# Two attention passes of a graph network: one-hots of the open nodes compared once, the fall factors finished by ScalarE, and scores less maxima formed by TensorE in PSUM

## The reference, cut to what matters

```python
m = jax.ops.segment_max(score, dst, num_segments=n)
ex = jnp.exp(score - m[dst])
denom = jax.ops.segment_sum(ex, dst, num_segments=n)
agg = jax.ops.segment_sum(ex[..., None] * message, dst, num_segments=n)
out = agg / denom[..., None]
```

## Time and profile before

| | |
|---|---|
| median of 3 runs | 3441.07 us (3435.51 to 3443.51) |
| span of the profiled execution, first to last instruction | 3438.5 us |
| VectorE's adds of pass 1 (416) | from 1399.9 to 1975.9 us |
| VectorE's adds of pass 2 (416) | from 2172.7 to 2737.0 us |
| TensorE busy in the span | 2897.5 us (84%) |
| VectorE, ScalarE, GpSimd busy | 2544.3 (74%), 1935.0 (56%), 2183.2 us (63%) |

### The profile page before, as it was taken

The page is one execution under the profiler, slowest core; times in us unless marked ns, Lnnn a source line. Parts: engine busy times, 40 slices in busy tenths (PEclk is TensorE's granted clock), DMA queues, the critical chain, the costliest instruction groups (busy, mean ns, idle before and its releaser), DMA issues. The chain is left out here.

```text
span 3438.5 us, 60509 instructions
## 1 busy us (share of the span) xinstructions
PE 2897.5 (84%) x15715; PEld 1839.2 (53%) x15715; DVE 2544.3 (74%) x6536; ACT 1935.0 (56%) x6284; POOL 2183.2 (63%) x2289
## 2 busy tenths in 40 slices
PE   5799889999988896788888866899999897788875
PEld 4666555555555553455555544677777653333332
DVE  8899789999977554888888843799999874444444
ACT  0478655555541452687788722688888753333333
POOL 1777677777756532766666355777777314777774
PEclk9999899999999998798899988899999996655665
DMA  5334388888851789777777555777777444333334
GB/s 179 100 104 130 121 256 261 260 265 264 261 138 34 242 324 351 243 229 220 218 209 212 128 186 184 224 227 227 228 228 226 117 199 162 104 103 103 103 104 103
DMA packets 260604, 651.44 MB, mean 189 GB/s; under 512 B 66781, under 2 KB 115626, under 8 KB 253498
## 3 DMA queue, kind: packets, MB, share of 16 engines
q0 software_dynamic: 141840, 474.50, 45.9%
q1 hardware_dynamic: 118442, 173.08, 15.5%
HBM read 505.42 MB, written 145.27 MB: 189 GB/s over the span
## 5 line engine op out<-in xcount | busy, mean ns | idle before, releaser
L2132 POOL DMA_INDIRECT a_rows<-table,met x568 | 560.3, 987 | 241.1 <-issue 137.8
L3729 PE MATMUL ps<-rows_in,hot_w 128*128 128x256 f32 x832 | 431.5, 630 | 114.2 <-ACT hot_w L3691 68.5
L1330 POOL DMA_INDIRECT rows_in<-table,met x416 | 413.1, 993 | 142.9 <-issue 80.3
L3679 POOL DMA_INDIRECT rows_in<-table,met x416 | 404.2, 972 | 144.3 <-issue 118.3
L3754 DVE TENSOR_TENSOR xs<-xs,ps 128x256 f32 x416 | 175.1, 421 | 302.7 <-PE ps L3729 298.1
L3729 PEld LDWEIGHTS ps<-rows_in,hot_w 128*128 128x128 f32 x832 | 192.6, 284 | 353.1 <-ACT hot_w L3691 199.2
L3691 ACT ACTIVATE hot_w<-hot,met 128x128 f32<-128x128 f32 x416 | 166.7, 402 | 372.1 <-PE ps L3729 353.9
L2629 PE MATMUL ps<-a_rows,a_hot 128*128 128x260 f32 x1136 | 316.4, 402 | 18.2 <-DVE acc L2635 12.7
L2132 POOL DMA_INDIRECT xs<-table,met x264 | 258.7, 980 | 107.3 <-issue 61.3
L833 POOL DMA_INDIRECT records<-rec,rows x241 | 260.5, 1081 | 87.6 <-issue 72.9
L2635 DVE TENSOR_TENSOR acc<-acc,ps 128x520 f32 x416 | 287.0, 690 | 34.6 <-PE ps L2629 13.6
(11 more groups left out here) (492 smaller groups left out, 6417.3 us busy)
## 6 DMA issues: line engine op xcount, KB each, us to landing
a_hot_t<-one_hots SPq DMA_DIRECT2D x104, 256.0 KB, 5.0
table<-stage SPq DMA_DIRECT2D x25, 1024.0 KB, 3.9
rows_in<-table,met POOLq DMA_INDIRECT x832, 3.8
one_hots<-hot_t SPq DMA_DIRECT2D x52, 256.0 KB
dst_row<-slot_rows SPq DMA_DIRECT2D x51, 256.0 KB, 5.0
by_dst<-dst_rows SPq DMA_DIRECT2D x25, 512.0 KB, 5.7
by_dst<-lo_rows SPq DMA_DIRECT2D x24, 512.0 KB, 4.4
a_rows<-table,met POOLq DMA_INDIRECT x568, 3.8
```

Of the source, the lines that this page charges most:

```text
L1330: e.indirect_dma_start(self.rows[:, n % self.RING, 0:2 * D], None, self.table, bass.IndirectOffsetOnAxis(ap=self.b.met[:, n, R_SRC:R_SRC + ...
L2132: e.indirect_dma_start(self.row(n, 0, self.width), None, self.table, bass.IndirectOffsetOnAxis(ap=b.met[:, n, self.word:self.word + 1], ax ...
L3679: e.indirect_dma_start(self.rows[:, n % self.RING, :], None, self.table, bass.IndirectOffsetOnAxis(ap=self.b.met[:, n, R_REL:R_REL + 1], a ...
L3729: e.matmul(b.ps[:, n % self.BANKS, 0:D], self.hot_w[:, n % GRP_H, :], self.rows[:, n % self.RING, :], start=True, stop=True).then_inc(self ...
```

## The change

1. `vector_ends` compares the 26 open nodes with all 128 partitions once (`opened[:, 0]`) and keeps one less that beside it (`opened[:, 1]`). The row of nodes is loaded to 128 partitions in place of 8. The comparison in each window on VectorE (`open`) and `other` on ScalarE are gone.
2. `scale_up` is one matmul: a matrix of ones times `diag`, which puts exp(-fall) on all partitions.
3. ScalarE finishes the factor in slot 0: factor = PSUM * opened0 + opened1, from PSUM to SBUF. It waits for `scale_out` (TensorE) and for the `rescaled` of the window before; `rescale` on VectorE waits for it and reads SBUF.
4. "back" on TensorE is two matmuls into one PSUM region in place of a transpose: identity times scores, then the maxima times minus the identity. `below` on VectorE is gone, and ScalarE takes the exponential from PSUM, behind `turned_back`.
5. Turning the scores of window w into the same bank now waits for the exponentials of window w-1 (`exped`), and the write of scores waits for "back" of window w-2.

```diff
 # Segments
-        self.opens = sb("opens", [H2, NW])
+        self.opened = sb("opened", [P, 2, NW])
...
-        e.tensor_copy(self.opens[:, :], self.local_f[:, 0:NCH:WIN]).then_inc(kept, 1)
+        e.tensor_scalar(self.opened[:, 0, :], self.local_f[:, 0:NCH:WIN], b.part_f[:, :], None, ALU.is_equal).then_inc(kept, 1)
         e.wait_ge(kept, 4)
+        e.tensor_scalar(self.opened[:, 1, :], self.opened[:, 0, :], -1.0, 1.0, ALU.mult, ALU.add)
...
-        e.dma_start(self.local_f[:, :], on_all(self.ends[2], H2)).then_inc(self.back, 16)
+        e.dma_start(self.local_f[:, :], on_all(self.ends[2], P)).then_inc(self.back, 16)
 # Attend.constants_vector
+        e.tensor_scalar(self.minus[:, :], b.ident[0:R, 0:R], -1.0, None, ALU.mult)
 # Attend.vector, add
-                e.wait_ge(self.scale_out, self.w0 + w + 1)
+                e.wait_ge(*self.factored.at(w + 1))
                 if n:
                     e.wait_ge(self.added, self.c0 + n)
-                self.rescale(e, tile, b.ps[:, self.SMALL, 128:128 + H]).then_inc(self.rescaled, 1)
+                self.rescale(e, tile, self.factor[:, :]).then_inc(self.rescaled, 1)
 # Attend.vector, chain
-                d0 = seg.opens[0:H, w:w + 1]
-                if w:
-                    e.wait_ge(self.scale_out, self.w0 + w)
-                step("open", e.tensor_scalar(self.open_hot[:, :], b.iota[0:H, :], d0, None, ALU.is_equal))
...
-            if at == here["below"]:
-                if w:
-                    e.wait_ge(self.exped, self.w0 + w)
-                e.wait_ge(self.turned_back, self.w0 + w + 1)
-                step("below", e.tensor_tensor(self.below[:, :], self.score[:, w % 2, :], b.ps[:, self.BACK, 0:R], ALU.subtract))
 # Attend.scalar
-                if w < NW and i == self.OTHER_AT:
-                    e.wait_ge(self.chain, self.chained(w, "open"))
-                    e.activation(self.other[0:1, :], self.open_hot[0:1, :], ACT.Identity, scale=-1.0, bias=self.b.ones[0:1, 0:1])
+                if n >= 0 and i == self.FACTOR_AT:
+                    now = self.seg.opened[:, :, w - 1:w]
+                    e.wait_ge(self.scale_out, self.w0 + w)
+                    if w > 1:
+                        e.wait_ge(self.rescaled, self.w0 + w - 1)
+                    e.activation(self.factor[:, :], self.b.ps[:, self.SMALL, 128:128 + H], ACT.Identity, scale=now[:, 0, :],
+                                 bias=now[:, 1, :]).then_inc(self.factored.sem, 1)
...
-                    e.wait_ge(self.chain, self.chained(w, "below"))
+                    e.wait_ge(self.turned_back, self.w0 + w + 1)
                     for k, m, s in self.pieces(w):
-                        last = e.activation(self.weights(s, m), self.scores_of(self.below, k, m), ACT.Exp)
+                        last = e.activation(self.weights(s, m), self.scores_of(self.b.ps[:, self.BACK, 0:self.rows_n], k, m), ACT.Exp)
 # Attend.tensor, chain
                 e.wait_ge(self.scored, self.scored_by(w))
+                if w:
+                    e.wait_ge(self.exped, self.w0 + w)
...
-                e.transpose(b.ps[:, self.BACK, 0:R], self.most_2[:, :], b.ident[0:R, 0:R]).then_inc(self.turned_back, 1)
+                e.matmul(b.ps[:, self.BACK, 0:R], b.ident[:, :], self.score[:, w % 2, :], start=True, stop=False)
+                e.matmul(b.ps[:, self.BACK, 0:R], self.most_2[:, :], self.minus[:, :], start=False, stop=True).then_inc(self.turned_back, 1)
 # Attend.tensor, scale_up
-            e.matmul(small[:, 128:128 + H], self.open_hot[:, :], self.diag[:, :], start=True, stop=False)
-            e.matmul(small[:, 128:128 + H], self.other[0:1, :], b.ones[0:1, 0:H], start=False, stop=True).then_inc(self.scale_out, 1)
+            e.matmul(small[:, 128:128 + H], b.ones[0:H, :], self.diag[:, :], start=True, stop=True).then_inc(self.scale_out, 1)
 # Attend1 (Attend2 alike, with OTHER_AT 8)
-    TURNS, HOT_AT, OTHER_AT = {"score": 5, "ends": 7, "spread": 10, "back": 12}, 3, 10
+    TURNS, HOT_AT, FACTOR_AT = {"score": 5, "ends": 7, "spread": 10, "back": 12}, 3, 0
...
-            e.wait_ge(self.chain, self.chained(w - 2, "below"))
+            e.wait_ge(self.turned_back, self.w0 + w - 1)
```

More of the change, by code:

```diff
@@ L1984, in open_tables @@
         self.segs = lent[0:CP, at:3 * at].bitcast(BF16).rearrange("c (g m q) -> c g m q", g=CG, m=4)
-        self.first, self.last, self.local_f = (lent[0:H2, 3 * at + k * NCH:3 * at + (k + 1) * NCH] for k in range(3))
+        self.first, self.last, self.local_f = (lent[0:n, 3 * at + k * NCH:3 * at + (k + 1) * NCH] for k, n in enumerate((H2, H2, P)))
         self.local_0 = b.sb("seg_local0", [CP, CG], F32, own)
@@ L2013, in vector_ends @@
     def vector_ends(self, e):
-        kept, finish = self.kept, self.finish
+        b, kept, finish = self.b, self.kept, self.finish
         e.wait_ge(self.back, 16 * 3)
@@ L2063, in __init__ @@
         self.mask = sb("mask", [R, 2, 4, P], BF16)
-        self.score, self.below = sb("score", [P, 2, R]), sb("below", [P, R])
+        self.score, self.minus = sb("score", [P, 2, R]), sb("minus", [R, R])
         self.run, self.most, self.most_1, self.most_2 = (sb(n, [R, P]) for n in ("run", "most", "most_1", "most_2"))
@@ L2072, in __init__ @@
         self.fall, self.keep_r, self.diag = sb("fall", [H, 1]), sb("keep_r", [H, 1]), sb("diag", [H, H])
-        self.open_hot, self.other = sb("open_hot", [H, P]), sb("other", [H, P])
+        self.factor = sb("factor", [P, H])
         self.hot_in, self.mask_in = [sem(f"hot_in{k}") for k in range(self.HOTS)], [sem("mask_in0"), sem("mask_in1")]
@@ L2081, in __init__ @@
         self.summed, self.added, self.rescaled = sem("summed"), sem("added"), sem("rescaled")
+        self.factored = b.counted("act_5", NW)
         self.prep = b.sem(f"{name}_constants")
     HOTS = 6
-    STEPS = ("run", "most", "ends_in", "open", "carry", "onto", "lead", "past", "tail", "last_in", "through", "first",
-             "picked", "edge", "most_1", "most_2", "fall", "below")
+    STEPS = ("run", "most", "ends_in", "carry", "onto", "lead", "past", "tail", "last_in", "through", "first",
+             "picked", "edge", "most_1", "most_2", "fall")
     def in_order(self, table, ahead):
@@ L2449 @@
     FETCHES = {5: [(1, 0)], 7: [(1, 1)], 10: [(1, 2)], 13: [(1, 3)], 14: [(1, 4)], 15: [(1, 5)], 1: [(0, 6)], 2: [(0, 7)]}
-    TURNS, HOT_AT, OTHER_AT = {"score": 5, "ends": 7, "spread": 10, "back": 12}, 3, 10
+    TURNS, HOT_AT, FACTOR_AT = {"score": 5, "ends": 7, "spread": 10, "back": 12}, 3, 0
     CHAIN = {"run": (5, True), "most": (6, False), "ends_in": (6, True), "carry": (8, False), "lead": (8, True), "tail": (9, False),
-             "through": (9, True), "picked": (10, True), "most_1": (11, False), "fall": (11, True), "below": (12, False)}
+             "through": (9, True), "picked": (10, True), "most_1": (11, False), "fall": (11, True)}
     def __init__(self, b, seg, own, acc, table, q_parts):
@@ L2553 @@
     FETCHES = {8 + k: [(1, k)] for k in range(WIN // 2)}
-    TURNS, HOT_AT, OTHER_AT = {"score": 3, "ends": 7, "spread": 10, "back": 13}, 2, 8
+    TURNS, HOT_AT, FACTOR_AT = {"score": 3, "ends": 7, "spread": 10, "back": 13}, 2, 0
     CHAIN = {"run": (4, True), "most": (5, True), "ends_in": (6, True), "carry": (8, False), "lead": (8, True), "tail": (9, False),
-             "through": (9, True), "picked": (11, True), "most_1": (12, True), "fall": (13, False), "below": (14, False)}
+             "through": (9, True), "picked": (11, True), "most_1": (12, True), "fall": (13, False)}
     def __init__(self, b, seg, own, acc, table, parts, x):
@@ L2596, in score_vector @@
         e.wait_ge(self.product, w + 1)
+        if w >= 2:
+            e.wait_ge(self.turned_back, self.w0 + w - 1)
         e.scalar_tensor_tensor(self.score[:, w % 2, :], self.total[:, :], 0.2, self.total[:, :], ALU.mult, ALU.max).then_inc(self.scored, 1)
```

## The result

The changed kernel takes 3461.9 us (median of 4, 3458.4 to 3466.4), the kernel before, run beside it, 3438.3 (4 runs): ratio 1.0071, 95% interval 1.0059 to 1.0083, 24 us slower. A later set on another chip gave 1.0087 (1.0073 to 1.0100). The forecast was 3451, 10 us slower, in a range that reaches to 3469. The sign of the whole, the place (pass 1) and both waits in it were right. The size was short by more than half, and pass 2 went the other way; the time lies in the range because the range left room upward for the clock.

A forecast was written before the change was run, and what follows sets the result against it. No engine alone bounds the kernel: VectorE leads up to "back", TensorE behind it in 19 of 25 pass 1 windows. 3438.5 + 13 (pass 1) - 3.5 (pass 2) = 3448 span; median 2.6 above, 3451; range 3420 to 3469.

The forecast's parts named there:

- ScalarE's wait, pass 1: Slot 0, pass 1: waiting for the factor makes `total(4)` 0.7 to 1.0 us late; net +0.25 us a window in 19 windows.
- The two products: "back", pass 1: four records in place of the transpose cost +0.1 to +0.6 us, leaving about +0.3 in 19 windows.
- The clock: Pass 1: longer windows move TensorE's half-clock stretch, adding 0 to 20 us; 4 us taken.
- the two direct terms: Pass 1: factor wait 0.25 and "back" products 0.3 us in 19 windows, less 0.2 in 6: +9.3 us.
- `scale_up`: TensorE, pass 1: dropping the second matmul frees 0.2 to 0.3 us there but gives nothing, at most 0.2.
- Pass 2: Whole second pass: net -0.14 us a window, 25 times, -3.5 us, bounds -14 and +3; ScalarE's wait hidden.
- B: Both passes: VectorE loses two instructions a window and the products fit TensorE's gaps, not slower, 3422 us; chance 0.12.
- C: Pass 1: more TensorE work around the stall keeps its clock at 1.00, saving 27 us, 3415 us; chance 0.13.
- D: Whole kernel: the pieces cancel, time within 5 us of before; chance 0.15.

The follow-up runs named there:

- experiment 7: Kernel before with only the two products at "back" and the exponential from PSUM, factor path as before: 3465.3 us, ratio 1.0087 to before.
- Experiment 6: Kernel before with only the new factor part; "back" stays a transpose and `below` stays on VectorE: 3452.1 us, ratio 1.0050 to before.
- Experiment 9: Kernel before plus 8 idle fp32 products on TensorE ahead of the wait at "back" in pass 1: 3413.6 us, ratio 0.9934 to before.
- experiment 5: Changed kernel again, unaltered, beside the kernel before on one chip: 3467.3 us, ratio 1.0087.
- experiment 8: Changed kernel with the factor two slots later (one in pass 2) and the first "back" product ahead of the wait: 3449.8 us, ratio 1.0042 to before.
- experiment 10: Changed kernel plus 8 idle products ahead of the wait at "back" in pass 1, on a slower chip: 3883.4 us, ratio 1.0017 to before.
- experiment 1: Kernel before with only the new factor part, "back" and `below` as before, on a slower chip: 3918.8 us, ratio 0.9978 to before.

## Why the prediction was right, and where it was short

The windows of pass 1 show where the time went. A window is counted here from one `fall` on VectorE to the next (0.20 us behind "back"), and cut at `scale_up` and at `run`; the table has the means of 21 windows of each profile, from about 1455 us on (20 in experiment 7, where one could not be cut). Windows in which TensorE is at half clock for 5.6 to 7.2 us are called long, those with 3.0 to 5.0 us short.

| kernel | kind | windows | to `scale_up` | to `run` | to `fall` | sum, us |
|---|---|---|---|---|---|---|
| before | long | 8 | 7.16 | 7.03 | 9.15 | 23.34 |
| before | short | 13 | 5.91 | 7.42 | 9.17 | 22.51 |
| changed | long | 20 | 7.38 | 7.39 | 9.18 | 23.96 |
| changed | short | 1 | 6.34 | 7.38 | 9.43 | 23.15 |
| factor alone (6) | long | 12 | 7.13 | 7.34 | 9.21 | 23.68 |
| factor alone (6) | short | 9 | 5.87 | 7.68 | 9.15 | 22.70 |
| "back" alone (7) | long | 20 | 7.71 | 7.05 | 9.14 | 23.89 |
| before, filled (9) | no half clock | 21 | 4.86 | 7.74 | 9.16 | 21.76 |

**ScalarE's wait, pass 1: right, with its size.** `total(4)` is 0.71 us late (0.7 to 1.0 said), the factor takes 0.35 us (0.30 and 0.2 were the bounds), `run` comes 0.30 us later behind `scale_up` (0.3 to 0.6 said; 0.36 in the means), and ScalarE catches up before slot 14. The 0.2 us that `open` was to give back can't be seen: from `run` to `fall` it is 9.15 us before and 9.18 now. So the term is 0.36 where 0.25 was put. Experiment 6 has this part alone: +11 us in pass 1.

**The two products: right in kind, and in this window near their size.** TensorE leads behind "back" there: its granted clock is 0.50 from 1713 to 1715 and 1.00 from 1717.5, and at 1718.40 VectorE waits 0.72 us for its sums. At half clock the transpose and the way to the next load took 0.39 us, and the four records take 1.23: +0.84 against at most +0.6. That most of it is made up once the clock is back fits: from `fall` to `scale_up` +0.22 are left, where 0.3 was put. The half-clock stretch did not grow with the products: by the clock records it is 6.83 us long in both windows read, from 1710.26 before and from 1716.77 now. Alone, in experiment 7, the part at "back" leaves +0.55 in the same place. Why it leaves less beside the factor isn't known.

**The clock: the term that was too small.** I took 4 us out of 0 to 20 for windows that lengthen because the half-clock stretch lies differently in them. By the table, long windows took 23.34 us before and 23.96 now: +0.62, near the 0.55 of the two direct terms. But 13 of 21 windows were short before and took 0.83 us less; now there is one. These 12 windows in 21, at 0.83 us, are some 12 us in 25 windows (an estimate from the table), three times what I took. The other 14 of the 26 us are the direct terms, which I had at 9. I had misread the rows of before in three places. The 22.2 us for an average window is a pass divided by 26, while the windows themselves take 22.8; and the bound of 20 us came from a difference of 1.65 us, which stands in no row (the table has 0.83). Nor do 13.8 us make 19 waits of 0.72: the row counts 33, 0.42 each in the mean. Experiment 9 shows that the price of stall and clock is real; experiments 6 and 7 show that it isn't additive: 11 and 24 us alone, 26 together. With the part at "back" alone, every window that could be cut is already a long one, and the factor's wait adds only 2 us to the pass. In the clock records every change of the clock lies on a grid of 3.41 us, and the half-clock stretches of pass 1 are 3.41 or 6.83 us long, 15 and 10 of them before, 3 and 22 now. That windows change kind because longer windows shift against this grid fits all of this, but no run varied the shift by itself; this part is argued, not shown.

**`scale_up`: right.** One matmul fewer gave nothing that shows.

**Pass 2: wrong in sign, by 6 to 9 us.** -3.5 was said, between -14 and +3; +5.1 came, and +2.8 in experiment 5. Two terms failed: the products cost 0.39 and not 0.3, and the 0.2 that VectorE's freedom from `below` was to give TensorE is 0.03 in the windows read, because the sums were what it waited for. -0.2 for `open`, which stands as inferred, + 0.39 - 0.03 leaves +0.16, 4 us in 25 windows. Experiment 7 confirms the place: +4.8 with the part at "back" alone.

**The rivals.** B (VectorE's relief decides) fell: VectorE has 5 and 12 us less to do and the passes are longer. C (the clock stays up) did not happen: it is 0.87 in pass 1. But experiment 9, with idle products in the stall, has it at 1.00, and brings the 27 us in pass 1 that C was priced at, nearly (25). One product ahead of the wait (experiment 8) isn't enough: the clock of its pass 1 is 0.89. D (the pieces cancel, within 5 us) fell with the 24 us.

**What stays open.** What the change costs with the clock held at 1.00, and whether it then pays, since experiment 10 ran on a chip where this can't be read. What the waits on those chips are. Why the half-clock stretch is longer in some windows than in others. The best version measured is that of experiment 9.

## What to carry to other kernels

Before work is taken from an engine, look which engine leads at that place: VectorE lost two instructions a window, and TensorE, which got the work, led there. A stall of TensorE cost twice here, once in itself and once in the clock of what follows (0.90 in pass 1, 1.00 without the stall): behind a 2.15 us stall, 5.05 us of work took 7.43, though with both gone the long windows shrank by 1.6 us only (23.34 to 21.76), since from `scale_up` to `run` they took 0.7 longer. Filling the stall with idle products was worth 24 us, more than any edit of the work here; whether it pays on the slower chips wasn't measured. Two edits that lengthen the same window are not added up: here 11 and 24 us made 26. An instruction that waits in the middle of an engine's list is priced by what is queued behind it: here `total(4)` came 0.71 us late. Moving it by two slots halved that wait (experiment 8: 3.5 to 1.6 us).

## What the runs showed that was not expected

- Idle products that nobody reads made the kernel 0.66% faster (ratio 0.9934), by holding TensorE's granted clock at 1.00 in a pass where it was 0.90.
- The two fp32 products at "back" take 0.45 us from load to next load at a granted clock of 1.00 (2430.70 to 2431.15 in pass 2) and 1.23 at 0.50 (1717.72 to 1718.95 in pass 1), a factor of 2.7 and not 2, though those of pass 1 have half the columns.
- The same kernel takes 3437 to 3438 us on some chips and 3874 or 3926 on two others, with waits for which the profile shows no work, up to 4.4 us in experiment 1 (TensorE's loads, 1700 to 2200), and small changes weigh differently there: the factor part alone is 0.9978 on one of them and 1.0050 on the others.
